# Attention and gated projection on eight cores: transposes with two buffers in flight, accumulator rows shared between VectorE and GpSimd, and PSUM banks alternated in two projections

## The chip, the cores and the metric

The kernel runs on the 8 cores of one Trainium2 chip, the same program on each with other data. Each core has five engines that take their instructions in order from a queue of their own: TensorE (PE in the rows), VectorE (DVE), ScalarE (ACT), GpSimd (POOL) and SyncE (SP). SP and ACT also issue DMAs. The metric is the device time of the slowest core in microseconds (us). Lower is better.

## The reference

For four sequences of 4096 rows with 4096 features, float32 in and out:

```
xn = layernorm(x)
q = (xn @ Wq) as 32 heads of 128;  k, v = halves of xn @ Wkv (one head, shared by all)
scores = q k^T / sqrt(128) + alibi bias, causal;  attn = softmax(scores)
s = concat_heads(attn @ v) @ Wo
g = silu(xn @ W^T + bias),  W = qweight * scales + scaled_zeros (int32 values, groups of 128)
out = x + s * g
```

## The kernel before

Two cores share a sequence. Each core owns two slots of 1024 query rows (s = 0 and 1); a slot's keys are a window of 2048 or 4096 rows that ends with it. The program is written by hand as a list of `P.emit(engine, instruction, waits, incs)`: each engine executes its own in the order written, and waits are on counters. "t", "v", "s" and "g" count what TensorE, VectorE, ScalarE and GpSimd have finished; each DMA stream has a counter of its own. `P.barrier()` makes every engine wait for all counters. The stages, in order:

- A: layernorm of all rows, written as bf16 to `xnh` in HBM.
- B (the K and V projection): three halves of 2048 rows. For each of 32 feature blocks j a DMA transpose brings 128 features of 2048 rows into `xnt[j % 2]`, and 8 matmuls of 512 columns (four 512-row chunks, once for K at L377, once for V at L383) add it into `pbigB`, which fills PSUM. That is 96 transposes and 768 matmuls. Transposes of even j are issued by SP, those of odd j by ScalarE (L373). Each waits for `("t", mm_done)`, the last matmul of the feature block before it, whichever buffer that one used.
- C: the Q projection, two halves of 32 output tiles. Its matmuls (L471) alternate between two parts of PSUM.
- D: dequantization and transposition of the second weight, and a bf16 copy of Wo.
- E, for each slot s: attention, then the Wo projection, then the gated projection (FFN).
- F: the final add.

Attention works on a block of 512 queries (qc = 0, 1) and on pairs of heads (i = 0, 1). A step is one tile of 128 keys. For each head of the pair TensorE multiplies Q and K (L684) into one of two banks, with a second matmul for bias or mask on some tiles (L690, L696); ScalarE takes the exponential (L709, L714) into one of two buffers `ppb` of that head; TensorE multiplies V with it (L654); and VectorE adds it into `accA` (float32, 128 x 512 for each head; the first step copies, L659, the others add, L664). An exponential waits for the matmul and for the `accA` operation that read the same `ppb` buffer two steps earlier (`pp_free`). There are 64 pairs with 783 steps in all; 745 steps have both heads, 38 only head i = 1. After a pair, for i = 0 and then i = 1: a matmul sums `accA` over partitions (L725), VectorE takes a reciprocal of 512 elements in one partition (L730) and casts it (L733), a matmul spreads it over the partitions (L737), and VectorE copies it (L742) and scales the output (L747).

The Wo projection has 32 output tiles, each of 64 matmuls (L767) into banks `pb_[0]` and `pb_[1]`, one evacuated by VectorE (L772), one by ScalarE (L775), then written to `sth`. A NO_OP on TensorE at L783 waits for both evacuations before the next tile. The FFN has 32 tiles of 64 matmuls (L815) into `pb_[2]` and `pb_[3]`; they wait for `prev_sil`, the activation (L822) of the tile before. VectorE multiplies the result with the s rows (L827), and ScalarE issues the store. On SP, the weights of tile ot (L803, waits for the multiply of tile ot-2) are followed by the s rows of tile ot (L807, wait for the multiply of tile ot-1).

Of the kernel before, what the change touches and what calls it, by code (L numbers as in the profile page):

```python
# [206 lines left out]
def build_nc(stop_phase=9, taps=(), dparts=('vtr', 'dq', 'wo')):  # L207
    nc = bass.Bass("TRN2", target_bir_lowering=False)
    P = Prog()
# [145 lines left out]
    with ExitStack() as stB2:  # L355
# [9 lines left out]
        mm_done = 0  # L365
        for s in range(2):
            e_s = SLOT_E[s]
            row0 = (QR if s == 0 else QR + SLOT_E[0])
            for half in range(e_s // 2048):
                r0h = row0 + 2048 * half  # L370
                for j in range(32):
                    pb = j % 2
                    dl = P.emit(("sync", "scalar")[pb], lambda e, jj=j, p_=pb, r0=r0h: e.dma_start_transpose(  # L373
                        xnt[p_][:, 0:2048], xnh[r0:r0 + 2048, 128 * jj:128 * (jj + 1)]),
                        waits=[("v", vcast), ("t", mm_done)], incs=[(f"bX{pb}", 16)])
                    for ch in range(4):
# [11 lines left out]
                            incs=[("t", 1)])  # L388
                wv = ws = 0
# [209 lines left out]
    with ExitStack() as stE:  # L599
# [12 lines left out]
        for s in range(2):  # L612
# [6 lines left out]
            for qc in range(2):  # L619
# [21 lines left out]
                for g2 in range(16):  # L641
# [9 lines left out]
                    def flush_avd():  # L651
                        for (i_p, ppi_p, jj_p, ex_p, st_p, sp_p) in pend:
# [4 lines left out]
                                waits=[("s", ex_p), bank_free[4 + i_p]], incs=[("t", 1)])  # L657
                            if st_p:
                                ac = P.emit("vector", lambda e, pi=ppi_p, i_=i_p: e.tensor_copy(  # L659
                                    out=accA[:, 512 * i_:512 * (i_ + 1)],  # L660
                                    in_=ppb[:, 512 * pi:512 * (pi + 1)]),
                                    waits=[("s", ex_p), acc_guard[i_p]], incs=[("v", 1)])
                            else:
                                ac = P.emit("vector", lambda e, pi=ppi_p, i_=i_p: e.tensor_tensor(  # L664
                                    out=accA[:, 512 * i_:512 * (i_ + 1)],
                                    in0=accA[:, 512 * i_:512 * (i_ + 1)],
                                    in1=ppb[:, 512 * pi:512 * (pi + 1)], op=ALU.add),
                                    waits=[("s", ex_p), last_ac[i_p]], incs=[("v", 1)])
                            last_ac[i_p] = ("v", ac)
# [86 lines left out]
            prevWo = {}  # L756
            for ot in range(32):
# [17 lines left out]
                e2 = P.emit("scalar", lambda e, p_=pbu: e.copy(  # L775
                    stsl[p_][:, 512:1024], pb_[1][:]),
# [6 lines left out]
                P.emit("tensor", lambda e: e.nop(), waits=[("v", e1), ("s", e2)])  # L783
# [13 lines left out]
            prev_sil = 0  # L797
            for ot in range(32):
                pbu = ot % 2
                waits = []  # L800
                if pbu in prevF:
# [7 lines left out]
                    waits=[("v", prev_mulf)], incs=[(f"eR{pbu}", 16)])  # L809
                mmf = 0  # L810
                for gg in range(32):
                    buf = attnT[gg // 16]
                    coff = 1024 * (gg % 16)
                    for q_ in range(2):
                        mmf = P.emit("tensor", lambda e, g_=gg, qq=q_, p_=pbu, b_=buf, c_=coff: e.matmul(  # L815
                            pb_[2 + qq][:], wftsl[p_][:, 128 * g_:128 * (g_ + 1)],
                            b_[:, c_ + 512 * qq:c_ + 512 * (qq + 1)],
                            start=(g_ == 0), stop=(g_ == 31)),
                            waits=[P.dw(f"eF{pbu}"), ex_full, ("s", prev_sil)], incs=[("t", 1)])
                sil = 0  # L820
                for q_ in range(2):
                    sil = P.emit("scalar", lambda e, o_=ot, qq=q_: e.activation(  # L822
                        gtsl[:, 512 * qq:512 * (qq + 1)], pb_[2 + qq][:], AF.Silu,
                        bias=c_fb[:, o_:o_ + 1]),
                        waits=[("t", mmf), ("v", prev_mulf)], incs=[("s", 1)])
                prev_sil = sil
# [96 lines left out]
```

How the kernel before makes its waits and increments, by code:

```python
                    def body(eng):  # L168
                        for (_e, waits, fn, incs) in my_evs:
                            for (sname, v) in waits:
                                eng.wait_ge(sem_handles[sname], v)
                            ins = fn(eng)
                            for (sname, n) in incs:
                                ins.then_inc(sem_handles[sname], n)
```

## Time and profile before

| | |
|---|---|
| median of 3 runs | 7974.12 us (7959.12 to 7979.56) |
| profiled execution, its own time | 7923.7 us |
| span of its slowest core (core 5) | 7922.2 us (all cores 7871.2 to 7922.2) |
| granted TensorE clock, mean | 0.81 |
| busy: TensorE, VectorE, ScalarE, GpSimd | 56%, 32%, 23%, 0% |
| stage B | 737 to 1494 us |
| attention, slot 0 and slot 1 | 3530 to 4437 us, 5475 to 6552 us |
| Wo projection, slot 0 and slot 1 | 4437 to 4930 us, 6552 to 7045 us |
| FFN with its transposes, slot 0 and slot 1 | 4930 to 5475 us, 7045 to 7600 us |

The stage limits are read from the timeline. Rows of the timeline give start and length in us, the engine, the line, and in square brackets how long the engine had been idle before and what ended that. PE rows show a matmul from its start to its modelled end, so neighbouring ones overlap: how fast they go is read from start to start.

### The profile page before, as it was taken

Reading aid. Unit: us, or ns where it says so; the run is one execution under the profiler, and the core shown is the slowest. Engines: PE = TensorE matmul, PEld = TensorE weight load, DVE = VectorE, ACT = ScalarE, POOL = GpSimd, SP = SyncE. Lnnn points to the kernel's source line nnn. Section 1 sums busy time; section 2 is a strip of 40 time slices with the busy share of each in tenths; the row PEclk is TensorE's granted clock in tenths of the full one; section 3 lists DMA queues with packets and bytes.
Section 4 is the critical chain, followed back from the end, with each engine's and each line's share of the span. In section 5 each row is a group of like instructions: output and inputs, shape, how many; then the busy total and the mean of one; then the engine's idle time right before and its main releaser. Section 6 shows DMA issues by size and latency. Waiting matters only on the chain.

```text
span 7922.2 us, 55853 instructions; the slowest of 8 cores (7871.2 to 7922.2 us)
## 1 busy us (share of the span) xinstructions
PE 4454.2 (56%) x18152; PEld 1779.5 (22%) x18152; DVE 2495.8 (32%) x3355; ACT 1803.6 (23%) x2712; POOL 0.2 (0%) x4
## 2 busy tenths in 40 slices
PE   0001444377669822106656798797675678969930
PEld 0000111133224422001211343333121123423310
DVE  4443000011100044327878300001897890000012
ACT  6774000000000044103535200001363470000000
POOL 0000000000000000000000000000000000000000
PEclk9999565588889955557767899899787789989975
DMA  7775333577763377990000233543000003354478
GB/s 271 292 298 209 66 67 69 106 163 158 159 123 96 98 208 210 278 327 2 1 26 1 58 87 87 109 103 94 1 1 26 1 1 84 87 104 100 101 183 277
DMA packets 1553327, 936.99 MB, mean 118 GB/s; under 512 B 1331602, under 2 KB 1487250, under 8 KB 1520018
## 3 DMA queue, kind: packets, MB, share of 16 engines
q1 hardware_dynamic: 1143954, 623.00, 31.1%
q10 hardware_dynamic: 409088, 310.41, 12.9%
q8 instruction: 152, 2.49, 0.1%
q14 instruction: 133, 1.09, 0.0%
HBM read 581.01 MB, written 251.66 MB: 105 GB/s over the span
## 4 chain that ended last, share of the span: by engine, by line
PE 47%; DMA 22%; DVE 15%; ACT 8%; issue 5%; SPq 3%; DVEq 0%; ACTq 0%
PE pbE L815 11%; PE pbE L767 11%; PE pqC L471 9%; DVE rd_f L730 5%; DMA xntB<-xnh 5%; DMA wqrC<-wq 4%; DMA xA<-xkv 3%; DMA wobh<-wobD 3%; DMA xcF<-xq 3%; ACT wfoD L535 3%; PE pbE L684 2%; DVE accA L664 2%; ACT ppb L709 2%; PE pbE L654 2%; PE pbigB L377 2%
## 5 line engine op out<-in xcount | busy, mean ns | idle before, releaser
L471 PE MATMUL pqC<-xntqC,wqbC 128*128 128x512 bf16 x4096 | 928.5, 390 | 327.4 <-DVE wqbC L452 266.9
L815 PE MATMUL pbE<-attnTE,wftslE 128*128 128x512 bf16 x4096 | 899.9, 381 | 215.9 <-DMA wftslE<-wfth 119.5
L767 PE MATMUL pbE<-attnTE,woslE 128*128 128x512 bf16 x4096 | 898.7, 380 | 99.8 <-DVE stslE L772 81.2
L709 ACT ACTIVATE ppb<-pbE,bslE 128x512 bf16<-128x512 f32 x1264 | 763.3, 712 | 571.2 <-PE pbE L684 562.4
L664 DVE TENSOR_TENSOR accA<-accA,ppb 128x512 f32<-128x512 f32 x1400 | 869.1, 685 | 61.4 <-ACT ppb L709 31.6
L377 PE MATMUL pbigB<-xntB,wkv_bf 128*128 128x512 bf16 x384 | 236.8, 617 | 1152.8 <-DMA xntB<-xnh 1152.8
L684 PE MATMUL pbE<-qtsE,kt 128*128 128x512 bf16 x1528 | 581.5, 438 | 378.6 <-DMA tsbE<-tstk 378.6
L654 PE MATMUL pbE<-ppb,vt 128*128 128x512 bf16 x1528 | 558.0, 403 | 74.1 <-ACT ppb L709 21.7
L471 PEld LDWEIGHTS pqC<-xntqC,wqbC 128*128 128x128 bf16 x4096 | 407.9, 100 | 848.5 <-issue 395.8
L815 PEld LDWEIGHTS pbE<-attnTE,wftslE 128*128 128x128 bf16 x4096 | 397.5, 98 | 718.3 <-issue 253.1
L767 PEld LDWEIGHTS pbE<-attnTE,woslE 128*128 128x128 bf16 x4096 | 397.2, 98 | 601.3 <-issue 135.3
L730 DVE RECIPROCAL rd_f<-pbE 1x512 f32<-1x512 f32 x128 | 428.2, 3346 | 61.4 <-PE pbE L725 61.3
L827 DVE TENSOR_TENSOR sgslE<-gtslE,stslE 128x1024 bf16<-128x1024 bf16 x64 | 44.3, 692 | 1074.4 <-ACT gtslE L822 1074.4
L301 DVE TENSOR_REDUCE stA<-xA 128x1 f32<-128x4096 f32 x64 | 282.9, 4420 | 295.9 <-DMA xA<-xkv 204.8
L737 PE MATMUL pbE<-rd_b,c_oner 1*128 1x512 bf16 x128 | 73.2, 572 | 526.9 <-DVE rd_b L733 526.9
L477 DVE CAST qstC<-pqC 128x512 bf16<-128x512 f32 x64 | 44.3, 692 | 975.1 <-PE pqC L471 975.1
L377 PEld LDWEIGHTS pbigB<-xntB,wkv_bf 128*128 128x128 bf16 x384 | 52.8, 138 | 1311.5 <-issue 1311.5
L772 DVE CAST stslE<-pbE 128x512 bf16<-128x512 f32 x64 | 44.3, 692 | 952.8 <-PE pbE L767 952.8
L555 PE MATMUL pbfD<-c_ident,wfoD 128*128 128x128 bf16 x1024 | 129.4, 306 | 357.8 <-ACT wfoD L535 265.1
L480 ACT CAST qstC<-pqC 128x512 bf16<-128x512 f32 x64 | 37.5, 586 | 1217.0 <-PE pqC L471 1217.0
L684 PEld LDWEIGHTS pbE<-qtsE,kt 128*128 128x128 bf16 x1528 | 158.9, 106 | 571.9 <-issue 481.4
L822 ACT ACTIVATE gtslE<-pbE,c_fb 128x512 bf16<-128x512 f32 x128 | 81.0, 684 | 883.1 <-PE pbE L815 883.0
(49 smaller groups left out, 2792.0 us busy)
## 6 DMA issues: line engine op xcount, KB each, us to landing
xA<-xkv SPq DMA_DIRECT2D x48, 2048.0 KB, 10.7
xnh<-xnA ACTq DMA_DIRECT2D x64, 1024.0 KB, 10.9
wqrC<-wq SPq DMA_DIRECT2D x32, 2048.0 KB, 17.8
qwD<-qw SPq DMA_DIRECT2D x32, 2048.0 KB, 8.8
worD<-wo SPq DMA_DIRECT2D x32, 2048.0 KB, 14.5
woslE<-wobh SPq DMA_DIRECT2D x64, 1024.0 KB, 8.8
wftslE<-wfth SPq DMA_DIRECT2D x64, 1024.0 KB, 9.5
xA<-xq SPq DMA_DIRECT2D x16, 2048.0 KB, 12.0
```

The source lines that it names most:

```text
L301: v1 = P.emit("vector", lambda e, p_=pb, st=st_: e.reduce_sum(out=st[:, 0:1], in_=xb[p_][:], axis=AX.X), waits=[P.dw(f"aX{pb}")], incs=[(" ...
L377: P.emit("tensor", lambda e, jj=j, p_=pb, c_=ch: e.matmul(pbig[:, 512 * c_:512 * (c_ + 1)], wkv_bf[:, 256 * jj:256 * jj + 128], xnt[p_][:, ...
L471: mm_done = P.emit("tensor", lambda e, jj=j, c_=ch, p_=pb: e.matmul(pq[:, 2048 * p_ + 512 * c_:2048 * p_ + 512 * (c_ + 1)], wqb[p_][:, 128 ...
L535: ws = P.emit("scalar", lambda e, o_=ot, g_=gg, p_=pb: e.activation(wfo[p_][:, 128 * g_:128 * (g_ + 1)], qwb[p_][:, 128 * g_:128 * (g_ + 1 ...
L555: trs = P.emit("tensor", lambda e, gg=g_, hf=half, uu=u, p_=pb: e.transpose(pbf[:, 1024 * hf + 128 * uu:1024 * hf + 128 * (uu + 1)], wfo[p ...
L654: st_=st_p, sp_=sp_p: e.matmul(pb_[4 + i_][:], vt_s[s_][:, 128 * jj:128 * (jj + 1)], ppb[:, 512 * pi:512 * (pi + 1)], start=st_, stop=sp_),
L664: ac = P.emit("vector", lambda e, pi=ppi_p, i_=i_p: e.tensor_tensor(out=accA[:, 512 * i_:512 * (i_ + 1)], in0=accA[:, 512 * i_:512 * (i_ + ...
L684: st1=not (near or diag): e.matmul(pb_[b_][:], kt_s[s_][:, 128 * jj:128 * (jj + 1)], qts[:, 512 * h_:512 * (h_ + 1)], start=True, stop=st1),
L709: ex = P.emit("scalar", lambda e, b_=sb, pi=ppi, f_=fi, j_=j: e.activation(ppb[:, 512 * pi:512 * (pi + 1)], pb_[b_][:], AF.Exp, bias=bsl[: ...
L730: rc = P.emit("vector", lambda e, i_=i: e.reciprocal(out=rd_f[i_][:], in_=pb_[6 + i_][0:1, :]), waits=[("t", dmm), ("v", rcb_guard[i])], i ...
L767: mmw = P.emit("tensor", lambda e, h_=ht, qq=q_, p_=pbu: e.matmul(pb_[qq][:], wosl[p_][:, 128 * h_:128 * (h_ + 1)], attnT[qq][:, 512 * h_: ...
L815: mmf = P.emit("tensor", lambda e, g_=gg, qq=q_, p_=pbu, b_=buf, c_=coff: e.matmul(pb_[2 + qq][:], wftsl[p_][:, 128 * g_:128 * (g_ + 1)], ...
```

## The change

- Stage B: all transposes are issued by SP. The transpose of block j waits for the matmuls of block j-2 (the last user of its buffer), counted through the three halves without a break by `gj`.
- Attention: the `accA` operations of head i = 1 are executed by GpSimd with the counter "g"; those of head i = 0 stay on VectorE.
- Wo projection: tiles alternate between banks 0, 1 and banks 4, 5; the NO_OP is gone, and the first matmul of a tile waits for the evacuations of tile ot-2.
- FFN: tiles alternate between banks 2, 3 and banks 6, 7, and the matmuls wait for the activation of tile ot-2.

```diff
@@ stage B
+        mmj_done = {}
+        gj = [0]
...
-                    pb = j % 2
-                    dl = P.emit(("sync", "scalar")[pb], lambda e, jj=j, p_=pb, r0=r0h: e.dma_start_transpose(
+                    pb = gj[0] % 2
+                    dl = P.emit("sync", lambda e, jj=j, p_=pb, r0=r0h: e.dma_start_transpose(
                         xnt[p_][:, 0:2048], xnh[r0:r0 + 2048, 128 * jj:128 * (jj + 1)]),
-                        waits=[("v", vcast), ("t", mm_done)], incs=[(f"bX{pb}", 16)])
+                        waits=[("v", vcast), ("t", mmj_done.get(gj[0] - 2, 0))],
+                        incs=[(f"bX{pb}", 16)])
...
+                    mmj_done[gj[0]] = mm_done
+                    gj[0] += 1
@@ attention, flush_avd
+                            eng, sn = (("vector", "v"), ("gpsimd", "g"))[i_p]
                             if st_p:
-                                ac = P.emit("vector", lambda e, pi=ppi_p, i_=i_p: e.tensor_copy(
+                                ac = P.emit(eng, lambda e, pi=ppi_p, i_=i_p: e.tensor_copy(
...
-                                    waits=[("s", ex_p), acc_guard[i_p]], incs=[("v", 1)])
+                                    waits=[("s", ex_p), acc_guard[i_p]], incs=[(sn, 1)])
                             else:
-                                ac = P.emit("vector", lambda e, pi=ppi_p, i_=i_p: e.tensor_tensor(
+                                ac = P.emit(eng, lambda e, pi=ppi_p, i_=i_p: e.tensor_tensor(
...
-                                    waits=[("s", ex_p), last_ac[i_p]], incs=[("v", 1)])
-                            last_ac[i_p] = ("v", ac)
+                                    waits=[("s", ex_p), last_ac[i_p]], incs=[(sn, 1)])
+                            last_ac[i_p] = (sn, ac)
@@ Wo projection
+            evac_guard = {0: [], 1: []}
...
+                bk = 4 * pbu
...
-                            pb_[qq][:], wosl[p_][:, 128 * h_:128 * (h_ + 1)],
+                            pb_[b_ + qq][:], wosl[p_][:, 128 * h_:128 * (h_ + 1)],
...
-                            waits=[P.dw(f"eW{pbu}")], incs=[("t", 1)])
+                            waits=[P.dw(f"eW{pbu}")] + evac_guard[pbu], incs=[("t", 1)])
...
-                P.emit("tensor", lambda e: e.nop(), waits=[("v", e1), ("s", e2)])
+                evac_guard[pbu] = [("v", e1), ("s", e2)]
@@ FFN
-            prev_sil = 0
+            sil_guard = {0: 0, 1: 0}
...
+                bkf = 2 + 4 * pbu
...
-                            waits=[P.dw(f"eF{pbu}"), ex_full, ("s", prev_sil)], incs=[("t", 1)])
+                            waits=[P.dw(f"eF{pbu}"), ex_full, ("s", sil_guard[pbu])],
+                            incs=[("t", 1)])
...
-                prev_sil = sil
+                sil_guard[pbu] = sil
```

The queue of SP in stage B, before. `xntB` is the transposed block, `xnh` the normalized rows in HBM, NO_OP a barrier:

```order
13 L155 NO_OP [waits sem_v,sem_s,sem_aC,sem_aX0,sem_aN0,sem_aX1,sem_aN1]
14 L361 DMA wkv_raw<-wkv 128x32x256
15 L373 DMA_TRANSPOSE xntB<-xnh 128x2048 [waits sem_v]
16 L373 DMA_TRANSPOSE xntB<-xnh 128x2048 [waits sem_t] x47
17 L155 NO_OP [waits sem_t,sem_v,sem_s,sem_bW,sem_bX0,sem_bX1]
```

and the queue of ScalarE there, before (CAST rows are the evacuations at the end of a half):

```order
322 L373 DMA_TRANSPOSE xntB<-xnh 128x2048 [waits sem_v,sem_t]
323 L373 DMA_TRANSPOSE xntB<-xnh 128x2048 [waits sem_t] x15
324 L401 CAST kt<-pbigB 128x512 [waits sem_t]
325 L405 CAST vtt<-pbigB 128x512
326 L401 CAST kt<-pbigB 128x512
327 L405 CAST vtt<-pbigB 128x512
328 L373 DMA_TRANSPOSE xntB<-xnh 128x2048 [waits sem_t] x16
```

The queue of SP in stage B now:

```order
13 L155 NO_OP [waits sem_v,sem_s,sem_aC,sem_aX0,sem_aN0,sem_aX1,sem_aN1]
14 L361 DMA wkv_raw<-wkv 128x32x256
15 L375 DMA_TRANSPOSE xntB<-xnh 128x2048 [waits sem_v]
16 L375 DMA_TRANSPOSE xntB<-xnh 128x2048
17 L375 DMA_TRANSPOSE xntB<-xnh 128x2048 [waits sem_t] x94
18 L155 NO_OP [waits sem_t,sem_v,sem_s,sem_bW,sem_bX0,sem_bX1]
```

All 96 transposes stand on SP, the first two with no wait on TensorE; ScalarE has only the evacuations left.

The queue of VectorE in attention, one pair of five steps, before (`accA` rows of both heads):

```order
702 L659 CAST accA<-ppb 128x512 x2
703 L664 TENSOR_TENSOR accA<-accA,ppb 128x512 x8
704 L730 RECIPROCAL rd_f<-pbE 1x512
705 L733 CAST rd_b<-rd_f 1x512
706 L742 COPY rs_f<-pbE 128x512
707 L747 TENSOR_TENSOR attnTE<-pbE,rs_f 128x512
```

VectorE in a pair of 16 steps now:

```order
812 L665 CAST accA<-ppb 128x512
813 L670 TENSOR_TENSOR accA<-accA,ppb 128x512 x15
814 L736 RECIPROCAL rd_f<-pbE 1x512
815 L739 CAST rd_b<-rd_f 1x512
816 L748 COPY rs_f<-pbE 128x512
817 L753 TENSOR_TENSOR attnTE<-pbE,rs_f 128x512
```

and GpSimd in the first pairs now (before, no such row stood on it):

```order
9 L665 CAST accA<-ppb 128x512 [waits sem_s]
10 L670 TENSOR_TENSOR accA<-accA,ppb 128x512 [waits sem_s,sem_g] x4
11 L665 CAST accA<-ppb 128x512 [waits sem_s,sem_t]
12 L670 TENSOR_TENSOR accA<-accA,ppb 128x512 [waits sem_s,sem_g] x4
13 L665 CAST accA<-ppb 128x512 [waits sem_s,sem_t]
```

One copy and n-1 adds of each pair of n steps stand on GpSimd; every add waits for ScalarE's exponential and for GpSimd's own add before it.

The queue of TensorE in the Wo projection before:

```order
2338 L767 MATMUL pbE<-attnTE,woslE 128x512 x63
2339 L783 NO_OP [waits sem_v,sem_s]
2340 L767 MATMUL pbE<-attnTE,woslE 128x512 [waits sem_eW1]
2341 L767 MATMUL pbE<-attnTE,woslE 128x512 x63
2342 L783 NO_OP [waits sem_v,sem_s]
```

and now:

```order
2340 L775 MATMUL pbE<-attnTE,woslE 128x512 x63
2341 L775 MATMUL pbE<-attnTE,woslE 128x512 [waits sem_eW0,sem_v,sem_s]
2342 L775 MATMUL pbE<-attnTE,woslE 128x512 x63
2343 L775 MATMUL pbE<-attnTE,woslE 128x512 [waits sem_eW1,sem_v,sem_s]
2344 L775 MATMUL pbE<-attnTE,woslE 128x512 x63
```

The wait for the evacuations stands on the first matmul of a tile and counts those of the tile before the last.

## Rows read from the trace of the kernel before

**Rows 1.** The page, busy us, share of the span, instructions of each engine
```profile
PE 4454.2 (56%) x18152; PEld 1779.5 (22%) x18152; DVE 2495.8 (32%) x3355; ACT 1803.6 (23%) x2712; POOL 0.2 (0%) x4
```

**Rows 2.** Windows by stage: stretch, its us, busy of each engine, clock, DMA share, GB/s
```profile
737.00:1494.00 757.00, 338.54 (x768) 98.89 (x768) 7.84 (x13) 6.16 (x12) 0.00 (x0) 0.60 0.30 67
2300.00:2747.00 447.00, 444.69 (x2048) 200.97 (x2048) 21.45 (x31) 18.17 (x31) 0.00 (x0) 0.99 0.37 92
3567.00:3973.00 406.00, 261.89 (x816) 77.94 (x816) 337.28 (x415) 176.59 (x307) 0.00 (x0) 0.76 0.00 1
4437.00:4930.00 493.00, 449.08 (x2048) 198.62 (x2048) 22.13 (x32) 18.76 (x32) 0.00 (x0) 1.00 0.35 83
4930.00:4985.00 55.00, 0.00 (x0) 0.00 (x0) 0.00 (x0) 0.00 (x0) 0.00 (x0) 0.50 1.00 175
4985.00:5475.00 490.00, 440.98 (x2002) 194.64 (x2003) 21.46 (x31) 40.54 (x63) 0.00 (x0) 0.99 0.47 100
```

**Rows 3.** Timeline of stage B: two transposes and the first matmuls of the blocks
```profile
1003.16 0.58 PE L377 MATMUL pbigB<-xntB,wkv_bf 128*128 128x512 bf16 x1 [4.41 <-DMA xntB<-xnh]
...
1006.80 2.01 SPq L373 DMA_TRANSPOSE xntB<-xnh  x1
1011.00 0.10 PEld L377 LDWEIGHTS pbigB<-xntB,wkv_bf 128*128 128x128 bf16 x1 [5.18 <-issue]
1011.03 0.59 PE L377 MATMUL pbigB<-xntB,wkv_bf 128*128 128x512 bf16 x1 [4.30 <-DMA xntB<-xnh]
```

**Rows 4.** Timeline, the 32 transposes of 1024 rows ahead of an FFN
```profile
4930.24 47.39 SPq L790 DMA_TRANSPOSE attnTE<-xnh  x32
```

**Rows 5.** Timeline of VectorE, the last pair of attention (32 steps)
```profile
6491.36 0.69 DVE L747 TENSOR_TENSOR attnTE<-pbE,rs_f 128x512 bf16<-128x512 f32 x1
6499.50 32.00 DVE L664 TENSOR_TENSOR accA<-accA,ppb 128x512 f32<-128x512 f32 x53
6532.16 3.35 DVE L730 RECIPROCAL rd_f<-pbE 1x512 f32<-1x512 f32 x1 [0.67 <-PE pbE L725]
6535.61 0.41 DVE L733 CAST rd_b<-rd_f 1x512 bf16<-1x512 f32 x1
6544.15 0.69 DVE L747 TENSOR_TENSOR attnTE<-pbE,rs_f 128x512 bf16<-128x512 f32 x1
```

**Rows 6.** Timeline of ScalarE in the same pair
```profile
6499.69 16.34 ACT L709 ACTIVATE ppb<-pbE,bslE 128x512 bf16<-128x512 f32 x28
```

**Rows 7.** Groups by line: count, busy us, mean ns, idle us before and releasers
```profile
L664 DVE TENSOR_TENSOR accA<-accA,ppb 128x512 f32<-128x512 f32 x1400 | 869.1, 685 | 61.4 <-ACT ppb L709 31.6 <-ACT ppb L714 23.0 <-DVE accA L664 4.8
L709 ACT ACTIVATE ppb<-pbE,bslE 128x512 bf16<-128x512 f32 x1264 | 763.3, 712 | 571.2 <-PE pbE L684 562.4 <-DVE accA L664 4.7 <-PE pbE L696 0.3
L730 DVE RECIPROCAL rd_f<-pbE 1x512 f32<-1x512 f32 x128 | 428.2, 3346 | 61.4 <-PE pbE L725 61.3
L208 POOL MEMSET const-bfloat16-1.0<- 128x1 bf16 x1 | 0.1, 101 | 0.0
```

**Rows 8.** The chain that ended last: start, us, what (Wo, FFN, Q projection)
```profile
4500.33 13.99 PE pbE L767 x64
4515.61 13.99 PE pbE L767 x64
5161.24 13.99 PE pbE L815 x64
5176.72 13.99 PE pbE L815 x64
...
2302.31 444.99 PE pqC L471 x2048
```

**Rows 9.** Timeline of the FFN around the start of one tile
```profile
5161.24 13.97 PE L815 MATMUL pbE<-attnTE,wftslE 128*128 128x512 bf16 x64 [1.51 <-ACT gtslE L822]
5161.33 0.69 DVE L827 TENSOR_TENSOR sgslE<-gtslE,stslE 128x1024 bf16<-128x1024 bf16 x1 [14.79 <-ACT gtslE L822]
5162.10 0.33 SPq L807 DMA_DIRECT2D stslE<-sth  x1
5162.47 0.43 SPq L803 DMA_DIRECT2D wftslE<-wfth  x1
```

**Rows 10.** DMA issues of the page: queue, count, KB each, median us to landing
```profile
woslE<-wobh SPq DMA_DIRECT2D x64, 1024.0 KB, 8.8
wftslE<-wfth SPq DMA_DIRECT2D x64, 1024.0 KB, 9.5
```

More of the change, by code:

```diff
@@ L766, in build_nc @@
                     for q_ in range(2):
-                        mmw = P.emit("tensor", lambda e, h_=ht, qq=q_, p_=pbu: e.matmul(
-                            pb_[qq][:], wosl[p_][:, 128 * h_:128 * (h_ + 1)],
+                        mmw = P.emit("tensor", lambda e, h_=ht, qq=q_, p_=pbu, b_=bk: e.matmul(
+                            pb_[b_ + qq][:], wosl[p_][:, 128 * h_:128 * (h_ + 1)],
                             attnT[qq][:, 512 * h_:512 * (h_ + 1)],
                             start=(h_ == 0), stop=(h_ == 31)),
-                            waits=[P.dw(f"eW{pbu}")], incs=[("t", 1)])
-                e1 = P.emit("vector", lambda e, p_=pbu: e.tensor_copy(
-                    out=stsl[p_][:, 0:512], in_=pb_[0][:]),
+                            waits=[P.dw(f"eW{pbu}")] + evac_guard[pbu], incs=[("t", 1)])
+                e1 = P.emit("vector", lambda e, p_=pbu, b_=bk: e.tensor_copy(
+                    out=stsl[p_][:, 0:512], in_=pb_[b_][:]),
                     waits=[("t", mmw), P.dw(f"eS{pbu}")], incs=[("v", 1)])
-                e2 = P.emit("scalar", lambda e, p_=pbu: e.copy(
-                    stsl[p_][:, 512:1024], pb_[1][:]),
+                e2 = P.emit("scalar", lambda e, p_=pbu, b_=bk: e.copy(
+                    stsl[p_][:, 512:1024], pb_[b_ + 1][:]),
                     waits=[("t", mmw), P.dw(f"eS{pbu}")], incs=[("s", 1)])
@@ L814, in build_nc @@
                     for q_ in range(2):
[L815 to L816 removed]
+                        mmf = P.emit("tensor", lambda e, g_=gg, qq=q_, p_=pbu, b_=buf, c_=coff,
+                                     bb=bkf: e.matmul(
+                            pb_[bb + qq][:], wftsl[p_][:, 128 * g_:128 * (g_ + 1)],
                             b_[:, c_ + 512 * qq:c_ + 512 * (qq + 1)],
                             start=(g_ == 0), stop=(g_ == 31)),
[L819 removed]
+                            waits=[P.dw(f"eF{pbu}"), ex_full, ("s", sil_guard[pbu])],
+                            incs=[("t", 1)])
                 sil = 0
                 for q_ in range(2):
[L822 to L823 removed]
+                    sil = P.emit("scalar", lambda e, o_=ot, qq=q_, bb=bkf: e.activation(
+                        gtsl[:, 512 * qq:512 * (qq + 1)], pb_[bb + qq][:], AF.Silu,
                         bias=c_fb[:, o_:o_ + 1]),
                         waits=[("t", mmf), ("v", prev_mulf)], incs=[("s", 1)])
[L826 removed]
+                sil_guard[pbu] = sil
                 mulf = P.emit("vector", lambda e, p_=pbu: e.tensor_tensor(
```

## The prediction

> **What bounds the kernel now.** I read the page first for the busy shares [rows 1]: no engine is above 56%, GpSimd is idle, so the time is a sum of stages with different limits. Then the windows by stage [rows 2] show where TensorE stands still and at which of its two clock levels it runs (0.50 is 1.2 GHz, 1.00 is 2.4 GHz). Then for each stage the change touches I read the timeline or the chain for the period of its loop and for what ends the wait in it.
>
> Stage B lasts 757 us with 339 us of TensorE busy and DMA engines 30% busy [rows 2]: neither is full. The timeline says why [rows 3]: from one block's first matmul to the next one's, 1003.16 to 1011.03, pass 7.87 us. TensorE's last matmul ends, at 1006.80 the next transpose starts on SP, and 4.23 us after that the matmuls start. Transfer and matmuls take turns: 96 x 7.87 = 755 us, the stage.
>
> Attention is paced by VectorE within a pair. In the last pair it does 53 adds in 32.00 us without a gap [rows 5], 0.604 us each, so 1.208 us per step of two heads. ScalarE is close behind: 28 exponentials in 16.34 us [rows 6], 0.584 each, 1.17 per step. At a pair's end comes a serial chain: from the end of the adds at 6531.50 to the end of the last scaling, 6544.84 [rows 5], 13.34 us, 3.35 twice of it reciprocals. The whole pair of 32 steps took 6544.84 - 6492.05 = 52.8 us; 32 x 1.208 + 13.34 = 52.0, so about 1.0 us more goes at its start. Before: a pair of n steps takes 1.208 n + 14.3. (With 146 steps in 16 pairs the first query block comes to 405 us; the window shows 406 [rows 2].)
>
> The Wo projection has a period of 4515.61 - 4500.33 = 15.28 us per tile, the FFN 5176.72 - 5161.24 = 15.48, for the same 64 matmuls at full clock [rows 8]. The gap is the evacuation that TensorE waits for [rows 9].
>
> **The change part by part.** All sums are made against the profiled execution, 7923.7 us; the median of the runs shown is 7974.1, 50 us more, and I add that at the end.
>
> *Stage B.* Both buffers may now be in use at once. Each buffer still goes through its own serial cycle of 7.87 us (transfer, then matmuls), but two such cycles interleave: 7.87 / 2 = 3.93 us per block. That is the slow end. It holds if nothing gets faster, and leaves TensorE busy 8 x 0.43 = 3.4 of 3.93 us, the 0.43 being the spacing at the lower clock. TensorE had a granted clock of 0.60 in this stage while it worked less than half of the time, and it is at 1.00 in stages where it is nearly always busy [rows 2], so I expect the clock to rise for part of it; that shortens the cycle by up to 1.7 us. The fast end is the transposes' own rate: 32 of 1024 rows left SP in 47.39 us [rows 4] with the DMA engines at 1.00 [rows 2], 1.48 us each, so 2.96 us for one of 2048 rows. SP's issue takes 2.0 us of it [rows 3] and is hidden. Between 2.96 and 3.93 I take the middle, 3.45: 96 x (7.87 - 3.45) = 424 us saved; ends 378 and 471. That ScalarE issues none any more is worth nothing: it is idle here.
>
> *Wo and FFN.* The Q projection's second half already alternates between two parts of PSUM and streams its weights likewise: 2048 matmuls in 444.99 us [rows 8], 13.91 us per 64. I take that as the new period. Wo: 31 gaps in each of 2 slots x (15.28 - 13.91) = 85 us. FFN: 62 x (15.48 - 13.91) = 97 us. What is late next: in Wo, the weights of the next tile are issued when the tile before the current one ends and land 8.8 us later [rows 10], 5 us early. In the FFN they are tighter. SP issues the weights of tile ot+1 behind the s rows of tile ot, which wait for the multiply of tile ot-1; that is 2.75 us after the matmuls of tile ot-1 end (5162.47 against 5161.24 - 1.51) [rows 9]. They land 9.5 us later in the median [rows 10], at 12.3 us; TensorE will want them at 13.9. The slack is 1.6 us, so the slowest landings show; I put 10 us on it (0 to 40). Together 85 + 87 = 172 us saved; ends 140 and 182.
>
> *Attention.* GpSimd gets 64 copies and 719 adds. Nothing in the trace shows what such an add costs there: its only rows are fills of one column, 0.10 us [rows 7], which say only that an instruction has some cost of its own. Bounds: it won't beat VectorE's 0.604 on the same operands, and the slowest pass over 512 columns in any row is the reciprocal, 3.35 us [rows 7]. The nearest row is VectorE's own add; I take twice that, 1.21 us: near the closest row, but on the dear side of it, as the other end is over five times as far. On top come two things. First, each GpSimd add waits for the one before it on the same accumulator, which VectorE hid by alternating between two accumulators; a dependent step costs 0.10 us, the gap between the reciprocal's end and the cast behind it [rows 5]. Second, both engines now run adds with two operands in SBUF side by side, and no row shows whether they hinder each other: between no hindrance and full turns I take full turns, which adds VectorE's 0.604. So a step takes P = 1.21 + 0.10 + 0.60 = 1.91 us.
>
> What this does to a pair: ScalarE's exponential for head 1 waits for GpSimd's add of two steps earlier, and stands in front of head 0's next one, so the whole pair moves at P. But GpSimd may be two adds behind at the end without harm, since head 0's half of the end chain (about 6.5 us) runs first and head 1's sum over partitions stands behind it on TensorE. So a pair takes about 0.7 us to the first tile of head 1, (n-2) P, 0.95 for the last exponential and the V matmul, and 13.3 for the chain: (n-2) P + 14.95. Against 1.208 n + 14.3 over 64 pairs and 783 steps the difference is 655 P - 904 us. P = 1.91 gives +347 us. If P falls below 1.3, ScalarE's 1.17 per step becomes the limit, and all that is won is 783 x 0.04 and some 0.6 us per pair: -68 us. That is the bound on the good side; at 3.35 + 0.10 + 0.60 = 4.05 the bound on the bad side would be +1750 us.
>
> For GpSimd the Trainium skill has a price that no run here shows: GPSIMD Engine Reference, section Elementwise — side-by-side cycle accounting, gives a two-input op about 2.6 cycles per element at 1.2 GHz. By that an add over 512 columns would be an estimated 1.11 us, P 1.81, and the whole time 7661 instead of the sum below. The skill's page SBUF — State Buffer, section Who interferes with whom, says a VectorE instruction with two SBUF inputs and a GpSimd instruction that reads SBUF fully block each other; by that the two adds take turns, which is the choice made above and the rule that speaks against this edit. No row of this trace can show it, GpSimd being idle.
>
> Sum: 7923.7 + 347 - 424 - 172 = 7675, and with the 50 us to the runs' median 7725 us (3.1% below 7974).
>
> **The rivals.**
>
> *No hindrance.* GpSimd and VectorE work side by side, P = 1.21 + 0.10 = 1.31. For it: no row shows a conflict, and ScalarE and VectorE overlap their passes over the same `ppb` tiles freely. Against it: nothing. Attention then costs 655 x 1.31 - 904 = -46 us, and the time is 7974 - 46 - 424 - 172 = 7332; with the -68 of the bound 7310.
>
> *GpSimd becomes the bound of the kernel (slower).* Place: the 719 adds of head 1. Price: three times VectorE's 0.604 in turns, or four times it without, P = 2.52: 655 x 2.52 - 904 = +747, time 7974 + 747 - 424 - 172 = 8125. It decides from P = (596 + 904) / 655 = 2.29, where the loss eats all that the other three edits save. For it: every step goes through this one dependent chain, and two adds is all the slack. Against it: the add would have to be over 2.6 times VectorE's.
>
> *The transposes don't overlap.* With all of them on one queue, a transpose might start only when the last has landed, or two in flight might slow each other so that the stage keeps over 7 us per block. It would save under 80 us, and the time would be near 8070. Against it: 32 of them left the same queue 1.48 us apart [rows 4], while one alone needs over 4 us to land [rows 3].
>
> **How the numbers follow.** Forecast (P from 1.6 to 2.2, all faster): 0.53. No hindrance or a quick GpSimd (P under 1.6): 0.22, all faster. GpSimd over 2.2: 0.20, of which 0.17 slower and 0.03 within the measurement. No overlap of the transposes: 0.05, slower. Faster 0.75, same 0.03, slower 0.22, where under 0.3% (24 us) is what a measurement of this kernel cannot tell from no change. The forecast's own range is P 1.6 to 2.2 with the ends of stage B: about 7480 to 7970. The range of 8 in 10 reaches down to the rival without hindrance and up to P = 2.4: 7300 to 8040.
>
> **What would show it.** Stage B 757 us shorter to about 335 us, with transposes on SP some 3.4 us apart, a granted clock above 0.60 and a DMA share above 0.6. Wo and FFN tiles 13.9 us apart, waits on VectorE and ScalarE gone from the matmuls, a small one on the weights' DMA left in the FFN. In attention, GpSimd rows of 1.1 to 1.3 us (or longer where they include a block), their starts 1.9 us apart in a long pair, ScalarE's exponentials waiting for GpSimd's add instead of TensorE, the two slots' attention of 1984 us grown to some 2330. The forecast is wrong if GpSimd's adds start under 1.5 or over 2.3 us apart, or if the transposes come over 4.5 us apart.

## The result

The changed kernel is faster: 7633.13 us median (7541.61 to 7883.50, 8 runs) against 7966.62 us for the kernel before on the same chips; ratio 0.952, 95% interval 0.948 to 0.957. Its profiled execution took 7563.2 us against 7923.7. A program on eight cores has some executions in which one die runs at a lower clock; the ratios compare only the others, so a ratio can differ from that of the medians.

Where the 361 us between the two profiles went. The stages are cut at marks on SP's queue: its first transpose or first weight DMA of each.

| stage | before, us | after, us | difference | forecast |
|---|---|---|---|---|
| B, K and V projection | 756.8 | 375.7 | -381 | -424 |
| C and D | 2055.0 | 2054.2 | -1 | 0 |
| attention, both slots | 1936.1 | 2140.0 | +204 | +347 |
| Wo projection, both slots | 1001.0 | 909.4 | -92 | -85 |
| FFN, both slots | 1118.9 | 1014.1 | -105 | -87 |
| A and F together | 1054.4 | 1068.3 | +14 | 0 |

Both columns are one core each, the slowest (core 5 before, core 3 after). Attention, Wo and FFN differ by 15 us at most between the cores. Stages C and D together take 2049 to 2084 us in the changed kernel depending on the core, so that differences of 10 to 20 us say nothing there. Stage B takes 342.6 to 357.1 us on the other seven cores and 375.7 on this one (before: 749.9 to 756.9 on all eight), so that seven cores saved 395 to 409 us in it.

### The profile page after: what moved, and what is told of

Read it like the earlier page. It is cut to its first block, busy times and chain, and to the rows that moved or that the text cites. A ratio compares the mean times of both kernels' runs of the same rounds, so it can differ in the third digit from the quotient of the medians.

```text
span 7561.6 us, 55969 instructions; the slowest of 8 cores (7492.5 to 7561.6 us)
## 1 busy us (share of the span) xinstructions
PE 4365.9 (58%) x18152; PEld 1766.9 (23%) x18152; DVE 2474.8 (33%) x2572; ACT 1830.8 (24%) x2712; POOL 1019.4 (13%) x787
## 4 chain that ended last, share of the span: by engine, by line
PE 44%; DVE 22%; DMA 21%; ACT 6%; issue 3%; SPq 3%; POOL 1%; DVEq 0%; ACTq 0%; POOLq 0%
PE pbE L775 12%; PE pbE L825 11%; PE pqC L476 10%; DVE accA L670 9%; DVE rd_f L736 6%; DMA wqrC<-wq 4%; DMA xA<-xkv 3%; DMA wobh<-wobD 3%; DMA xcF<-xq 3%; DMA xntB<-xnh 3%; ACT wfoD L540 3%; PE pbE L731 3%; PE pbE L690 2%; DVE stA L301 2%; PE pbfD L560 2%
## 5 line engine op out<-in xcount | busy, mean ns | idle before, releaser
L670 POOL TENSOR_TENSOR accA<-accA,ppb 128x512 f32<-128x512 f32 x719 | 980.2, 1363 | 176.1 <-ACT ppb L715 50.3
L715 ACT ACTIVATE ppb<-pbE,bslE 128x512 bf16<-128x512 f32 x1264 | 790.6, 686 | 726.0 <-PE pbE L690 608.0
L665 POOL CAST accA<-ppb 128x512 f32<-128x512 bf16 x64 | 39.0, 610 | 5056.4 <-ACT ppb L720 3181.7
L659 PE MATMUL pbE<-ppb,vt 128*128 128x512 bf16 x1528 | 581.3, 406 | 191.8 <-ACT ppb L715 157.0
L380 PE MATMUL pbigB<-xntB,wkv_bf 128*128 128x512 bf16 x384 | 170.3, 443 | 886.3 <-DMA xntB<-xnh 880.2
L659 PEld LDWEIGHTS pbE<-ppb,vt 128*128 128x128 bf16 x1528 | 155.2, 102 | 620.3 <-issue 576.2
```

The lines of the kernel that those rows point to most:

```text
L659: st_=st_p, sp_=sp_p: e.matmul(pb_[4 + i_][:], vt_s[s_][:, 128 * jj:128 * (jj + 1)], ppb[:, 512 * pi:512 * (pi + 1)], start=st_, stop=sp_),
L670: ac = P.emit(eng, lambda e, pi=ppi_p, i_=i_p: e.tensor_tensor(out=accA[:, 512 * i_:512 * (i_ + 1)], in0=accA[:, 512 * i_:512 * (i_ + 1)], ...
L715: ex = P.emit("scalar", lambda e, b_=sb, pi=ppi, f_=fi, j_=j: e.activation(ppb[:, 512 * pi:512 * (pi + 1)], pb_[b_][:], AF.Exp, bias=bsl[: ...
```

## The profile after

The page's first lines, as [rows 1] had them for before: GpSimd is now busy 13% of the span, and VectorE is as busy as ever although 719 adds have left it.

```profile
PE 4365.9 (58%) x18152; PEld 1766.9 (23%) x18152; DVE 2474.8 (33%) x2572; ACT 1830.8 (24%) x2712; POOL 1019.4 (13%) x787
```

Windows of stage B, of a Wo projection and of an FFN (columns as in [rows 2]):

```profile
732.80:1108.00 375.20, 219.37 (x768) 78.77 (x768) 7.23 (x12) 6.16 (x12) 0.00 (x0) 0.88 0.70 134
4125.00:4569.60 444.60, 444.07 (x2048) 200.86 (x2048) 21.46 (x31) 18.14 (x31) 0.00 (x0) 0.99 0.37 92
4630.00:5076.00 446.00, 443.97 (x2046) 200.56 (x2047) 21.45 (x31) 40.48 (x63) 0.00 (x0) 0.99 0.47 110
```

In stage B the clock is granted at 0.88 instead of 0.60 and the DMA engines are at 0.70 instead of 0.30. The timeline there, to set beside [rows 3]:

```profile
1002.21 0.38 PE L380 MATMUL pbigB<-xntB,wkv_bf 128*128 128x512 bf16 x1 [3.71 <-DMA xntB<-xnh]
...
1005.44 0.58 PE L380 MATMUL pbigB<-xntB,wkv_bf 128*128 128x512 bf16 x1 [0.90 <-DMA xntB<-xnh]
...
1009.29 0.58 PE L380 MATMUL pbigB<-xntB,wkv_bf 128*128 128x512 bf16 x1 [0.28 <-DMA xntB<-xnh]
...
1013.60 0.38 PE L380 MATMUL pbigB<-xntB,wkv_bf 128*128 128x512 bf16 x1 [1.92 <-DMA xntB<-xnh]
```

The blocks start 3.2, 3.9 and 4.3 us apart, 3.9 in the mean (375.7 / 96), and TensorE still waits for the transposes. A transpose now lands 4.8 us after its issue in the median, where it took 4.1. The other cores are quicker: 3.6 to 3.7 us per block, and on core 4 (342.6 us) a transpose lands after 4.5 us.

The chain that ended last in the Wo projection of slot 0 and the FFN of slot 1 (start, us, what), beside [rows 8]:

```profile
4125.53 444.45 PE pbE L775 x2048
...
6776.56 445.00 PE pbE L825 x2048
```

Both stages have become one unbroken run of 2048 matmuls, 13.89 and 13.91 us per tile. In the FFN of slot 0 the chain passes twice more through the weights' DMA after the start; TensorE stood still for 0.69 us and for 0.38 us. The first of the two:

```profile
4689.18 3.18 PE L825 MATMUL pbE<-attnTE,wftslE 128*128 128x512 bf16 x14 [0.69 <-DMA wftslE<-wfth]
```

Attention, by line (columns as in [rows 7]); the first two rows are the two halves of what was L664, the third is the matmul that sums the accumulator:

```profile
L670 POOL TENSOR_TENSOR accA<-accA,ppb 128x512 f32<-128x512 f32 x719 | 980.2, 1363 | 176.1 <-ACT ppb L715 50.3 <-ACT ppb L720 43.3 <-POOL accA L670 2.9
L670 DVE TENSOR_TENSOR accA<-accA,ppb 128x512 f32<-128x512 f32 x681 | 871.7, 1280 | 229.2 <-ACT ppb L715 97.6 <-ACT ppb L720 83.1 <-DVE accA L670 0.5
L731 PE MATMUL pbE<-accA,c_onecf 128*1 128x512 f32 x256 | 193.1, 848 | 55.1 <-DVE accA L670 55.1
```

VectorE's own add has gone from 685 ns [rows 7] to 1280. The last pair of 32 steps on ScalarE, then on VectorE and GpSimd (three answers of the timeline), beside [rows 5, 6]. The last ScalarE row is the last exponential of the pair, the last VectorE row its last scaling:

```profile
6225.97 1.26 ACT L715 ACTIVATE ppb<-pbE,bslE 128x512 bf16<-128x512 f32 x2 [0.30 <-POOL accA L670]
6227.52 1.26 ACT L715 ACTIVATE ppb<-pbE,bslE 128x512 bf16<-128x512 f32 x2 [0.29 <-POOL accA L670]
...
6249.39 0.69 ACT L715 ACTIVATE ppb<-pbE,bslE 128x512 bf16<-128x512 f32 x1 [0.29 <-POOL accA L670]
```
```profile
6207.96 43.44 DVE L670 TENSOR_TENSOR accA<-accA,ppb 128x512 f32<-128x512 f32 x28 [0.28 <-ACT ppb L715]
6252.68 3.35 DVE L736 RECIPROCAL rd_f<-pbE 1x512 f32<-1x512 f32 x1 [1.27 <-PE pbE L731]
...
6265.01 0.69 DVE L753 TENSOR_TENSOR attnTE<-pbE,rs_f 128x512 bf16<-128x512 f32 x1
```
```profile
6203.25 0.61 POOL L665 CAST accA<-ppb 128x512 f32<-128x512 bf16 x1 [14.21 <-ACT ppb L715]
6204.42 1.15 POOL L670 TENSOR_TENSOR accA<-accA,ppb 128x512 f32<-128x512 f32 x1 [0.56 <-ACT ppb L715]
...
6207.41 45.00 POOL L670 TENSOR_TENSOR accA<-accA,ppb 128x512 f32<-128x512 f32 x29 [0.28 <-ACT ppb L715]
```

ScalarE's pairs of exponentials, one pair per step, start 1.56 us apart (before, a step took 1.21), and what ends their wait is GpSimd's add. GpSimd's first add of the pair took 1.15 us. In the run of 29 the adds come 1.55 us apart (45.00 / 29). The timeline merges them into one row, but each starts 0.14 us after the end of the one before and is itself 1.42 us long; VectorE's adds beside them are 1.46 us long with 0.10 between. So in the middle of a long pair both engines show themselves busy nearly all the time.

## The experiments

The theory after the result: the three edits add up; the GpSimd edit costs about 204 us, because a GpSimd add (1.15 us) and a VectorE add that both read two operands in SBUF keep each other off. Rivals: GpSimd's dependent chain is that slow by itself; or any VectorE work beside it slows it; or part of the growth belongs to the other edits. Attention below is always the sum over both slots, between the same marks on SP's queue.

**no_pool**, the changed kernel without its GpSimd edit:

```diff
-                            eng, sn = (("vector", "v"), ("gpsimd", "g"))[i_p]
+                            eng, sn = ("vector", "v")
```

> The changed kernel with all accumulator operations back on VectorE. My theory: the GpSimd edit is a loss of the 204 us by which attention grew between the two profiles (1936 to 2140 us, from SP's queue marks), and it is independent of the other edits. So attention returns to about 1936 us with adds 0.604 us apart, stage B stays at 376 us, Wo and FFN at 13.9 us per tile, and the time is about 0.928 of the kernel before (7974 - 578 = 7396). Rival: part of the growth belongs to something else (banks, clock), then attention stays above 2000 us and the ratio nearer 0.94 to 0.95.

Measured: ratio 0.932 (0.918 to 0.946), profiled span 7360.5 us, attention 1929.6. The edit was a loss inside a gain. The last pair's adds are back at 58 in 35.18 us:

```profile
6015.92 35.18 DVE L670 TENSOR_TENSOR accA<-accA,ppb 128x512 f32<-128x512 f32 x58 [0.41 <-ACT ppb L715]
```

**pool_only**, the kernel before with that edit alone:

> The kernel before with the GpSimd edit alone. Theory: slower by about 204 us, ratio 1.026, steps of a long pair 1.56 us apart as in the changed kernel, stage B, Wo and FFN as before. Rival (the loss only appears together with the other edits): ratio within 1.00 to 1.01.

Measured: slower, ratio 1.034 (1.025 to 1.042). On core 6 attention takes 2142.7 us, 207 more than before, with the same durations as in the changed kernel; so the loss does not depend on the other edits. The ratio is above the 1.026 expected. In the profiled execution the slowest core, core 1, also took 641.6 us instead of 559.4 in the FFN of slot 1, which this edit does not touch, so the cost of the edit is read from attention, not from the ratio:

```profile
L665 POOL TENSOR_TENSOR accA<-accA,ppb 128x512 f32<-128x512 f32 x719 | 979.6, 1362 | 178.0 <-ACT ppb L710 50.7 <-ACT ppb L715 45.3 <-POOL accA L665 3.6
L665 DVE TENSOR_TENSOR accA<-accA,ppb 128x512 f32<-128x512 f32 x681 | 871.1, 1279 | 231.2 <-ACT ppb L710 95.7 <-ACT ppb L715 86.8 <-DVE accA L665 1.2
```

**lone_pool**, GpSimd's adds without VectorE's:

```diff
-                            if st_p:
+                            if i_p == 0:
+                                ac = P.emit(eng, lambda e: e.memset(accA[:, 0:512], 1.0),
+                                            waits=[acc_guard[0]], incs=[(sn, 1)]) if st_p else None
+                            elif st_p:
...
-                            last_ac[i_p] = (sn, ac)
+                            if ac is not None:
+                                last_ac[i_p] = (sn, ac)
```

> The changed kernel with the accumulator operations of head 0 left out (its accumulator is filled with ones once per pair), those of head 1 on GpSimd as they are; that part of the softmax sum is missing. Theory (the two engines' adds with two SBUF inputs take turns): GpSimd's add takes 1.15 us when VectorE is silent, starts 1.25 us apart or a little more, ScalarE nearly the limit at 1.17, attention about 1900 us, profiled time near 7310. Rival (GpSimd's dependent adds pace by themselves at 1.56): adds still 1.56 us apart, attention near 2140, time near 7560.

Core 7 is read, here and in the next one: span 7391.6 us (the same core of the changed kernel: 7557.2), attention 1959.6. GpSimd's adds take 1.15 us and start 37.44 / 29 = 1.29 us apart:

```profile
L673 POOL TENSOR_TENSOR accA<-accA,ppb 128x512 f32<-128x512 f32 x719 | 828.9, 1153 | 177.8 <-ACT ppb L719 58.4 <-ACT ppb L724 39.6 <-POOL accA L673 2.1
...
L668 POOL CAST accA<-ppb 128x512 f32<-128x512 bf16 x64 | 39.0, 610 | 5023.2 <-ACT ppb L724 3214.8 <-PE pbE L700 1299.6 <-ACT ppb L719 307.0
```
```profile
6032.17 37.44 POOL L673 TENSOR_TENSOR accA<-accA,ppb 128x512 f32<-128x512 f32 x29 [0.27 <-ACT ppb L719]
```

So GpSimd by itself is not what holds a step at 1.56. But even alone it is no gain: 1.29 per step is over VectorE's 1.21 for both heads, and attention stays 24 us above the kernel before. I had expected 1.25 and 1900. The 1.29 is GpSimd's own chain: each add starts 0.14 us after the end of the one before, and ScalarE's exponential starts between the two.

**one_sbuf**, VectorE's add kept, with one operand from PSUM:

```diff
+                            elif i_p == 0 and bank_free[6][0] == "v":
+                                ac = P.emit(eng, lambda e, pi=ppi_p, i_=i_p: e.tensor_tensor(
+                                    out=accA[:, 512 * i_:512 * (i_ + 1)],
+                                    in0=pb_[6][:],
...
```

> The changed kernel, but from the second pair of a slot on VectorE's add for head 0 reads a PSUM bank instead of the accumulator as its first input, so it has one SBUF input; length, engine and number of instructions stay, the sum of head 0 is not computed. Theory (only reads of the second SBUF operand exclude GpSimd): VectorE's add falls from 1.4 to about 0.69 us, GpSimd's from 1.42 to 1.15, starts about 1.25 us apart, attention about 1900 us, time near 7310. Rival A (any VectorE work beside GpSimd costs it): steps stay at 1.56. Rival B (GpSimd's own chain): also 1.56, and then the run without VectorE's adds shows 1.56 too.

Measured on core 7: span 7395.4 us, attention 1961.1. Both engines are back at the durations that they have without the other's adds beside them (1.15 us in lone_pool, 685 ns in [rows 7]):

```profile
L676 POOL TENSOR_TENSOR accA<-accA,ppb 128x512 f32<-128x512 f32 x719 | 831.7, 1157 | 177.0 <-ACT ppb L721 56.5 <-ACT ppb L726 38.8 <-POOL accA L676 3.5
...
L670 DVE TENSOR_TENSOR accA<-pbE,ppb 128x512 f32<-128x512 f32 x673 | 465.4, 692 | 451.5 <-ACT ppb L721 362.4 <-ACT ppb L726 88.8 <-DVE accA L670 0.2
```

This separates the theories. Same number of VectorE adds, same length, same engine, one SBUF operand less: VectorE's add falls from 1283 ns (same core of the changed kernel) to 692, GpSimd's from 1364 to 1157. Rivals A and B both fall. Such an add also no longer reads what the add before it wrote; no run separates that from the move of the operand to PSUM. I had expected 1.25 us and 1900 us here too; it came to 1.29 and 1961. The Trainium skill's page SBUF — State Buffer, section Who interferes with whom, says just this of two SBUF inputs; the runs agree on who hinders whom. They don't agree with full turns: 1.15 + 0.69 would be 1.84 us a step, or 1.75 with the 0.60 us at which VectorE's adds follow each other in [rows 5]. Measured is 1.56, so by this estimate 0.19 to 0.28 us of the two instructions overlaps.

**banks_only** and **banks_again**, the Wo and FFN edits alone on the kernel before (the same kernel, timed twice):

> The kernel before with the two PSUM edits (Wo and FFN) alone. Theory: the four stages lose the 197 us that separate the two profiles there (SP's queue marks), tiles 13.9 us apart, nothing else moves: 7974 - 197 = 7777, ratio 0.975. Rival (part of the saving needs the other edits, or TensorE's higher duty lowers the clock over a longer run): tiles over 14.2 us apart, ratio over 0.98.

> The same kernel as banks_only (the two PSUM edits alone), timed in more rounds. Theory (the edits' effects add up): its four stages lost 197 us in the profile, so a ratio of 0.975; rival (something of it is given back elsewhere): 0.98 to 0.99.

Measured: ratio 0.972 (0.965 to 0.979) for banks_again. The fastest run of banks_only, 7775 us, stands beside 7908 to 7960 us in the compared runs of the kernel before, which is 0.977 to 0.983; beside banks_again those took 7973 to 8055. So the ratio is good to about a hundredth, and the stages are the firmer evidence: in the profile of banks_again Wo and FFN take 454.8, 508.1, 455.2 and 506.6 us, 195 less than before, and attention stays at 1931. The two edits thus bring here what they bring in the changed kernel, and some 25 us more than the 172 of the forecast.

**three_buf**, no_pool with three transpose buffers in stage B:

```diff
-                    pb = gj[0] % 2
+                    pb = gj[0] % 3
...
-                        waits=[("v", vcast), ("t", mmj_done.get(gj[0] - 2, 0))],
+                        waits=[("v", vcast), ("t", mmj_done.get(gj[0] - 3, 0))],
```

> The kernel with all additions on VectorE, and in stage B three transpose buffers instead of two (block j waits for the matmuls of j-3). Theory 1: stage B is held at 3.7 to 3.9 us per block by the two-buffer cycle (landing 4.8 us after issue plus the matmuls); a third buffer takes that away and the transposes' own rate is left, 2.96 to 3.2 us per block, DMA share near 1.0, stage B 290 to 310 us instead of 352 to 376, time some 60 us less than without the third buffer (ratio near 0.92). Rival: the transposes on one queue are limited by something per transfer (issue on SP or HBM reads of all cores); then the stage stays at 350 us or more and SP's issues become longer while the DMA share stays near 0.7.

Measured: ratio 0.921 (0.915 to 0.927). That interval overlaps the one of no_pool (0.918 to 0.946), so the gain is read from the stage: it takes 288 to 306 us on the eight cores, where no_pool has 345 to 375. On core 7, the slowest, it is 306.2 us, 3.19 per block; the window of nearly all of it:

```profile
733.00:1033.00 300.00, 202.90 (x765) 76.02 (x766) 4.97 (x8) 4.11 (x8) 0.00 (x0) 0.91 0.96 168
```

The DMA engines are now at 0.96 and land a transpose after 5.8 us: with three buffers the transfers are the limit, with two, at a DMA share of 0.70, it was the cycle of a buffer.

**best**, three_buf with a short end of each pair of heads, and **best_scaled**, the same with a scale in the logarithm:

```diff
-                            pb_[6 + i_][0:1, :], c_onecf[:], accA[:, 512 * i_:512 * (i_ + 1)],
+                            pb_[6 + i_][:], c_onesf[:], accA[:, 512 * i_:512 * (i_ + 1)],
...
+                        lg = P.emit("scalar", lambda e, i_=i: e.activation(
+                            rl_f[i_][:], pb_[6 + i_][:], AF.Ln, scale=4294967296.0),
+                            waits=[("t", dmm), rs_guard[i]], incs=[("s", 1)])
+                        bank_free[6 + i] = ("s", lg)
+                        rcp = P.emit("scalar", lambda e, i_=i: e.activation(
+                            rs_f[i_][:], rl_f[i_][:], AF.Exp, scale=-1.0, bias=c_lnb[:]),
+                            waits=[("s", lg), rs_guard[i]], incs=[("s", 1)])
```

The lines are those of best_scaled; best has them without `scale=4294967296.0` and without `bias`. The reciprocal, cast, spreading matmul and copy fall away; `c_onesf` is a 128x128 tile of ones, `c_lnb` holds 32 ln 2. Each head also gets a buffer `rs_f` of its own, where both shared one.

> The kernel with three transpose buffers and all additions on VectorE, and a shorter end of a pair: the matmul that sums the accumulator uses a 128x128 tile of ones, so that the sum stands in all partitions, ScalarE forms the reciprocal as exp(-ln(sum)), and the cast, the spreading matmul and the copy fall away. Theory: attention's length is 783 steps plus 64 serial ends of 13.3 us, so shortening the end pays in full: sum 1.1, Ln and Exp 0.75 each, scaling 0.69, the second head behind it, about 4.9 us per pair instead of 13.3. That is 64 x 8.4 = 540 us: attention from 1930 to about 1390 us, time near 6800, ratio near 0.86. Rival: ScalarE's work for the next pair queues behind Ln and Exp, and a table load (1.28 us) is paid at every change of function: two loads per pair and a later start would leave 200 to 350 us of gain, ratio 0.88 to 0.90.

> The short pair end with the logarithm's input scaled by 2^32 and the factor taken back in the exponential's bias, since a far head's sum can be as small as exp(-53) by the bias that is left in it and the logarithm may not hold there. Theory: the values are then right and the timing is that of the unscaled form: attention about 1296 us, time near 6630, ratio 0.83 to 0.84. Rival: the scale or the bias operand makes Ln and Exp slower than 0.59 and 0.63 us, then attention over 1320 us.

Measured: best came to 6628.6 us in its fastest run, but it computes wrong values (relative error 0.043). With the scale and the bias as the only difference the values are right, so the range of the logarithm's input was the fault. best_scaled has a profiled span of 6645.3 us and attention of 1306.2 us. The same kernel timed again:

> The same kernel as best_scaled, timed in more rounds, since its first timing left too few comparable runs for an interval. All theories expect 6630 to 6670 us and a ratio of 0.835 to 0.845.

gave 0.832 (0.826 to 0.837), the fastest kernel of this study with right values. (Its runs of 6659 to 6671 us are 0.835 to 0.837 of the 7974 us at the start of this document; the compared runs of the kernel before took 7973 to 8055 beside it.) The last pair's end on VectorE in best_scaled:

```profile
5311.56 35.08 DVE L673 TENSOR_TENSOR accA<-accA,ppb 128x512 f32<-128x512 f32 x58 [0.41 <-ACT ppb L718]
5348.90 0.69 DVE L746 TENSOR_TENSOR attnTE<-pbE,rs_f 128x512 bf16<-128x512 f32 x1 [2.25 <-ACT rs_f L743]
5350.20 0.69 DVE L746 TENSOR_TENSOR attnTE<-pbE,rs_f 128x512 bf16<-128x512 f32 x1 [0.61 <-ACT rs_f L743]
```

From the end of the adds, 5346.64, to the end of the last scaling, 5350.89, pass 4.25 us instead of the 13.34 of [rows 5], with no table load in between. Attention gained 631 us over three_buf's 1937.5, more than 64 x 9.1 = 582. Summed over 62 of the 64 pairs, the ends became 561 us shorter and the stretches up to a pair's last add another 54, most of that in the short pairs (10.2 us instead of 11.6 in those of 5 steps, 39.1 and 39.2 in those of 32). The window of the last query block shows the clock at 0.95, where it is 0.80 in three_buf; that the clock is what speeds up the short pairs is not shown.

**dve_recip**, three_buf with the same tile of ones, but VectorE's reciprocal on all partitions:

> The same, but VectorE's reciprocal (3.35 us) on the sum in all partitions instead of Ln and Exp on ScalarE. It tells how much of the gain comes from leaving the cast, spread and copy out, and how much from taking 2 x 3.35 us off VectorE. Theory (the end is serial): per pair sum 1.1, twice reciprocal and scaling 2 x 4.1, so 9.3 us instead of 13.3: attention near 1930 - 64 x 4.0 = 1670 us, and some more if the next pair's matmuls start earlier; time near 7030, ratio 0.88 to 0.89. Rival (a reciprocal over 128 partitions is slower than over one): attention stays above 1750.

Measured: ratio 0.885 (0.882 to 0.888), attention 1670.7 us against 1670 expected. That it fits so closely is chance: the end of a pair takes 8.96 us instead of the 9.3 expected, and the stretches before it became some 11 us longer in all. A reciprocal of 512 columns takes 3.35 us over 128 partitions as over one. So of the 631 us, 267 come with leaving out the cast, spread and copy (and with the second `rs_f`), and 364 with moving the reciprocal to ScalarE.

## Why the prediction was right, point by point

The direction and the range were right, and so was the split: gains in stage B and in Wo and FFN, and a loss in attention that is smaller than they are. 7725 us was 92 us above the median, and three sizes were off. Between the two profiles the forecast was 112 us too slow, and the parts cancel in it: attention was forecast 143 us too dear and Wo and FFN 25 too poor, while stage B was forecast 43 too good and the untouched stages grew by 13. So the closeness of the sum is in part luck. One sign was missed: the forecast's own case was P, the time of one step in attention, between 1.6 and 2.2 us; the measured 1.56 lies just outside, in the case "a quick GpSimd" that had a chance of 0.22, though above the 1.5 at which the forecast called itself wrong.

One more row of the kernel before, the last 23 exponentials of its last pair, for the point on the formula:

```profile
6516.22 13.89 ACT L709 ACTIVATE ppb<-pbE,bslE 128x512 bf16<-128x512 f32 x23 [0.19 <-PE pbE L684]
```

- *Stage B: -424 forecast, -381 measured.* The two-buffer cycle was the mechanism, and so was the rise of the clock (0.60 to 0.88). The mis-sized term is the period, 3.45: I took the middle between 2.96 and 3.93, and measured is 3.91 on the slowest core, at the slow end, and 3.57 to 3.72 on the other seven. TensorE got faster, but a transpose that has another beside it takes longer: landing went from 4.1 to 4.8 us (4.5 on core 4). Why core 3 is behind the others is not settled. three_buf shows that the cycle was the limit: with a third buffer the period is 3.19 and the DMA share 0.96, though not the 2.96 that I had read off the shorter transposes.
- *Wo and FFN: -172 forecast, -197 measured.* The new period of 13.91 us, taken from the Q projection, was met (13.89 and 13.91). The old one was read off one gap of each; TensorE's total wait for the evacuations was 81.2 us in Wo and 96.3 in the FFN, and the matmuls' modelled tails, 0.16 us at each of 124 ends, make that 197. The 10 us put on late weights were two waits of 0.69 and 0.38 us.
- *Attention: +347 forecast, +204 measured.* The step that was mis-sized is P: 1.91 forecast, 1.56 measured. Its parts: the GpSimd add 1.21 forecast, 1.15 measured; the dependent wait 0.10 forecast, 0.14 measured (1.29 - 1.15 in lone_pool); VectorE's turn 0.60 forecast, 0.27 measured (1.56 - 1.29). So the term that failed is the turn, taken as full where the adds overlap in part. That 1.21 came so near to 1.15 was luck: it was twice VectorE's add, and no row spoke for the factor. The Trainium skill's price of 2.6 cycles per element (GPSIMD Engine Reference, Elementwise — side-by-side cycle accounting) gave an estimated 1.11, and the traces show 1.15.
- *The formula.* With P = 1.56 it gives 655 x 1.56 - 904 = +118, not +204. Its fixed term for the end of a pair is too small. After the end of the last exponential it leaves 0.95 - 0.69 for the V matmul and 13.3 for the chain, 13.6 us; the last pair took 6265.70 - 6250.08 = 15.6, and before, by [rows 5] and the row above, 6544.84 - 6530.11 = 14.7. So the formula had the end 1.1 us shorter than before where it became 0.9 longer. Part of the lengthening is that the last VectorE add of a pair is itself held up by GpSimd: it ended at 6251.40, and TensorE's sum waited for it, 55.1 us in all pairs, where before there were 4.2. But this is not the whole reason for the 86 us: lone_pool has no such wait, and the formula misses it by as much (P = 1.29 gives -59, measured is +24), with an end of 14.25 us in its last pair. In the other direction, a step takes 1.56 us only in the middle of long pairs (VectorE's adds are 1.28 us in the mean and 1.46 there), so that the formula overrates the steps. How the 86 us divide is not settled.
- *The rivals.* No hindrance would have left P at 1.29, which lone_pool and one_sbuf show as attention 24 us slower than before, not faster: its forecast of -46 came from the same formula with the same fault. GpSimd as the bound of the kernel needed P over 2.29. That the transposes don't overlap is refuted by their spacing: on one queue they come 3.91 us apart, and each lands 4.8 us after its issue.

## What to carry to other kernels

Before work is moved to GpSimd, compare its dependent step (here 1.29 us for an add over 512 columns) with what the busy engine pays for both shares (1.21): with two SBUF operands on each side the two engines also hinder each other, and in one_sbuf one operand in PSUM removed that. A change made of several edits can be faster and still hold a loss; undoing one at a time found 0.932 behind 0.952. And an end that recurs 64 times in series, 13.3 us each, was worth more here than any of the edits to the loops: cutting it to 4.25 brought attention 631 us, against 381 for stage B and 197 for Wo and FFN.

## What the runs showed of the hardware that was not expected

- A VectorE add with two SBUF operands and a GpSimd add don't take full turns: 1.56 us for one of each against 1.15 and 0.69 alone, while the profile shows them as 1.36 and 1.28 us busy in the mean, 1.42 and 1.46 in a long pair. So busy time grew by the hindrance, and a busier engine did no more work; whether such an instruction waits first or runs slower throughout, the rows don't show.
- VectorE's reciprocal takes 3.35 us for 512 columns on 1 and on 128 partitions; on ScalarE Ln (0.59 us) and Exp (0.72 with the bias) of the same 512 columns take 1.3, without a table load between them.
- A DMA transpose of 2048 rows by 128 columns of bf16 lands 4.1 us after issue with one in flight, 4.8 with up to two and 5.8 with up to three (medians of the slowest core), where one starts every 3.19 us and the DMA engines are at 0.96.
